# Attention times V on four 64x64 quarters in two turns, and a new order on every engine

## The reference

```python
q = rmsnorm((x @ wq.T).reshape(B, T, 16, 64), q_norm_w)
k = rmsnorm((x @ wk.T).reshape(B, T, 4, 64), k_norm_w);  v = (x @ wv.T).reshape(B, T, 4, 64)
scores = einsum('bqhd,bkhd->bhqk', q, repeat(k, 4)) / 8
mask = (i >= j) & (i - j < 128)
y = einsum('bhqk,bkhd->bqhd', softmax(where(mask, scores, -inf)), repeat(v, 4))
x = x0 + y @ wo.T                      # x above is layernorm(x0)
x = x + base(layernorm(x)) + gated_lora(layernorm(x))
```

## Time and profile before

| | |
|---|---|
| median of 3 runs | 2423.83 us (2421.53 to 2424.13) |
| profiled execution, its own time | 2420.27 us |
| its span, first to last instruction | 2418.6 us |
| TensorE, VectorE, ScalarE, GpSimd busy | 2380.1, 2152.0, 2160.9, 1309.6 us |
| granted TensorE clock, mean | 0.996 |
| bytes moved | 41.23 MB, mean 17 GB/s |

### The profile page before, as it was taken

The page is one execution under the profiler, slowest core; times in us unless marked ns, Lnnn a source line. Parts: engine busy times, 40 slices in busy tenths (PEclk is TensorE's granted clock), DMA queues, the critical chain, the costliest instruction groups (busy, mean ns, idle before and its releaser), DMA issues.

```text
span 2418.6 us, 70409 instructions
## 1 busy us (share of the span) xinstructions
PE 2380.1 (98%) x25856; PEld 1958.6 (81%) x25856; DVE 2152.0 (89%) x5736; ACT 2160.9 (89%) x7687; POOL 1309.6 (54%) x1771
## 2 busy tenths in 40 slices
PE   6999999999999999999999999999999999999997
PEld 4888888888888888888888888888888888888886
DVE  6899899999988999999999899989999998999886
ACT  5899989999998999899989989998999899899996
POOL 3555555555555555555555555555555555555542
PEclk9999999999999999999999999999999999999999
DMA  2000000000000000000000000000000000000000
GB/s 70 13 15 19 15 15 16 18 15 15 19 15 15 15 19 15 15 15 19 15 15 19 16 15 15 19 15 15 15 20 15 15 17 18 15 15 19 13 9 12
DMA packets 39729, 41.23 MB, mean 17 GB/s; under 512 B 4448, under 2 KB 38624, under 8 KB 39392
## 3 DMA queue, kind: packets, MB, share of 16 engines
q1 hardware_dynamic: 39392, 36.73, 5.0%
HBM read 19.93 MB, written 16.78 MB: 15 GB/s over the span
## 4 chain that ended last, share of the span: by engine, by line
PE 97%; issue 1%; ACT 1%; POOL 1%; DVE 1%; DMA 0%; SPq 0%; POOLq 0%
PE ps_a L633 17%; PE ps_scores L676 14%; PE ps_y L695 12%; PE ps_d L629 7%; PE ps_d L627 7%; PE ps_d L628 7%; PE ps_y L710 5%; PE ps_b L629 5%; PE ps_b L627 5%; PE ps_b L628 5%; PE ps_d L633 3%; PE ps_c L629 2%; PE ps_c L628 2%; PE ps_c L627 2%; PE ps_c L633 1%
## 5 line engine op out<-in xcount | busy, mean ns | idle before, releaser
L330 ACT ACTIVATE probs<-merged,neg_max 128x128 f32<-128x128 f32 x2048 | 796.0, 394 | 0.5 <-DVE neg_max L491 0.5
L253 POOL TENSOR_SCALAR_AFFINE_SELECT pT_other<-pT 128x256 f32<-128x256 f32 x384 | 173.1, 451 | 606.4 <-ACT pT L345 606.4
L237 POOL TENSOR_TENSOR q_r<-q_ve,minus_half 128x8 f32<-128x8 f32 x256 | 420.3, 1642 | 92.4 <-DVE q_ve L467 92.4
L676 PE MATMUL ps_scores<-kT,qT 64*64 64x192 f32 (+2 forms) x8192 | 415.2, 311 | 1.0 <-DVE merged L481 0.6
L330 ACT ACTIVATION_READ_ACCUMULATOR probs<-merged,neg_max 128x1 f32 x2048 | 396.5, 194 | 0.0
L481 DVE COPY_PREDICATED merged<-later_key,ps_scores 128x512 f32<-128x512 int32 x384 | 284.7, 741 | 106.2 <-ACT merged L323 106.2
L345 ACT ACTIVATE pT<-ps_a 128x512 f32<-128x512 f32 x512 | 306.2, 598 | 62.0 <-PE ps_a L633 61.1
L491 DVE TENSOR_REDUCE neg_max<-merged 128x4 f32<-128x512 f32 x512 | 346.5, 677 | 4.5
L695 PE MATMUL ps_y<-pT,values 128*64 128x128 f32 x4096 | 337.0, 285 | 1.8 <-ACT pT L345 1.8
L633 PE MATMUL ps_a<-ident,probs 128*128 128x128 f32 x2048 | 336.4, 287 | 0.0
L676 PEld LDWEIGHTS ps_scores<-kT,qT 64*64 64x64 f32 x8192 | 262.7, 133 | 60.6 <-issue 32.8
(11 more groups left out here) (114 smaller groups left out, 6175.7 us busy)
## 6 DMA issues: line engine op xcount, KB each, us to landing
xs<-x SPq DMA_DIRECT2D x128, 128.0 KB, 2.2
out<-ob SPq DMA_DIRECT2D x128, 128.0 KB, 1.7
w_plain<-w_qkv SPq DMA_DIRECT2D x3, 512.0 KB, 5.0
w_plain<-w_o SPq DMA_DIRECT2D x8, 128.0 KB, 5.3
w_plain<-w_ffn SPq DMA_DIRECT2D x1, 392.0 KB, 5.7
w_plain<-w_v SPq DMA_DIRECT2D x1, 128.0 KB, 4.9
nw<-norm_w SPq DMA_DIRECT2D x1, 1.0 KB, 5.5
```

The costliest lines, as they stand in the source:

```text
L237: pool.tensor_tensor(q_r[:, T % DEEP, c], q_ve[:, T % DEEP, c], minus_half[:, 0:8], ALU.pow).then_inc(s_qr[n], 1)
L330: last = nc.scalar.activation(probs[:, r, h], merged[:, r, h], ACT.Exp, bias=neg_max[:, r, h:h + 1], accum_out=den[:, r, h:h + 1])
L676: last = nc.tensor.matmul(ps_scores[queries, 2 * half + c, first:end], qT[rows, T % 2, 2 * g + c, queries], kT[rows, g // 2, at + first:at ...
```

## The change

The product with V is cut finer. What was one pass over 128 keys (`attend`) is now two turns of four matmuls over 64 keys, each on one quarter of the array: `attend_across`, the keys of the half that lies across from the queries' half, and `attend`, the keys of the same half. The first turn starts the sums in `ps_y`, then come the scores of a group of the next tile, then `attend` and `attend_other`, in one order or the other. The two later ones wait for the new semaphore `s_px`, which the first turn's last matmul raises. The number of multiplications is the same, the number of matmuls of L695 doubles.

```diff
-            def attend(T, g, first=True):
+            def attend_across(T, g):
                 pe.wait_ge(s_pT, groups(T, g))
...
-                for n in range(2):
-                    for half in range(2):
-                        last = nc.tensor.matmul(ps_y[HD * half:HD * half + HD, n, 0:P], values[:, T % WIDE, g // 2 * 2 + half],
-                                                pT[:, ring(T, g), 2 * half:2 * half + 2, HD * n:HD * n + HD], start=first, stop=ends, skip_group_check=True)
+                for half in range(2):
+                    for n in range(2):
+                        keys = slice(HD - HD * n, P - HD * n)
+                        last = nc.tensor.matmul(ps_y[HD * half:HD * half + HD, n, 0:P], values[keys, T % WIDE, g // 2 * 2 + half],
+                                                pT[keys, ring(T, g), 2 * half:2 * half + 2, HD * n:HD * n + HD], start=True, stop=False, skip_group_check=True)
+                last.then_inc(s_px, 1)
+
+            def attend(T, g, last=False):
+
+                pe.wait_ge(s_px, groups(T, g))
+                ends = last or not slot(T)
+                for half in range(2):
+                    for n in range(2):
+                        keys = slice(HD * n, HD * n + HD)
+                        end = nc.tensor.matmul(ps_y[HD * half:HD * half + HD, n, 0:P], values[keys, T % WIDE, g // 2 * 2 + half],
+                                               pT[keys, ring(T, g), 2 * half:2 * half + 2, HD * n:HD * n + HD], start=False, stop=ends, skip_group_check=True)
```

The lists of all five engines are new, the small PSUM banks are handed out anew, and the drain has one more step on TensorE. Of these lists two lines of VectorE and SyncE's loop:

```diff
-        ps_q, ps_qT = [ps_d, ps_c], [ps_d, ps_a]
-        ps_kv, ps_kT, ps_xT, ps_hT, ps_tT = ps_b, ps_a, ps_d, ps_a, ps_c
+        ps_q, ps_qT = [ps_d, ps_c], [ps_b, ps_a]
+        ps_kv, ps_kT, ps_xT, ps_hT, ps_tT = ps_c, ps_b, ps_a, ps_a, ps_a
...
-            for T in range(TILES):
+            for T in range(TILES + 2):
                 load_x(T + WIDE)
-                sp.wait_ge(s_ob, done(T))
-                sp.dma_start(out[T * P:(T + 1) * P, :], ob[:, T % 2]).then_inc(s_st[T % 2], 16)
+                store(T - 2)
...
-                x_statistics(T + 4)
...
+                add_x(T - 1)
+                x_statistics(T + 7)
```

More of the change, by code:

```diff
@@ L170, in load_x, with store @@
                     sp.dma_start(xs[:, T % WIDE], x[T * P:(T + 1) * P, :]).then_inc(s_x[T % WIDE], 16)
+            def store(T):
+                if live(T):
+                    sp.wait_ge(s_ob, done(T))
+                    sp.dma_start(out[T * P:(T + 1) * P, :], ob[:, T % 2]).then_inc(s_st[T % 2], 16)
             def load_weight(n):
@@ new lines, in step @@
+                norm_probs(T, 0)
+                k_mean_square(T + 1)
+                low_x(T + 2)
+                maximum(T, 2)
+                norm_h(T - 2)
+                inverse(T, 1)
+                norm_k(T + 1)
+                x_mean_and_var(T + 6)
+                low_y(T - 1, 3)
+                merge(T, 3)
+                norm_probs(T, 1)
+                maximum(T, 3)
+                inverse(T, 2)
+                sum_q(T + 1, 1)
+                low_h(T - 2)
+                q_mean_square(T + 1, 1)
@@ L618, in _ @@
+                add_x(T - 1)
+                x_statistics(T + 7)
+                h_statistics(T - 1)
+                high_value_difference(T + 1)
+                if T == -1:
+                    low_weights(W_FFN, W_O, W_V)
+                merge(T + 1, 0)
+                low_y(T, 0)
             low_weights(0, 1, 2)
@@ L709, in attend_other @@
                         keys = slice(HD * n, HD * n + HD)
-                        last = nc.tensor.matmul(ps_y[HD * half:HD * half + HD, n, 0:P], v_diff[keys, T % RING, g // 2 * 2 + half],
-                                                pT_other[keys, ring(T, g), n, 2 * half:2 * half + 2], start=first, stop=not first, skip_group_check=True)
-                if not first:
-                    last.then_inc(s_pv, 1)
+                        end = nc.tensor.matmul(ps_y[HD * half:HD * half + HD, n, 0:P], v_diff[keys, T % RING, g // 2 * 2 + half],
+                                               pT_other[keys, ring(T, g), n, 2 * half:2 * half + 2], start=False, stop=last, skip_group_check=True)
+                if last:
+                    end.then_inc(s_pv, 1)
             def project_out(T, g):
@@ new lines, in step @@
+                if live(T - 1):
+                    freed(pe, (s_merged, T - 1, groups(T - 1, 1)))
+                    scores(T - 1, 2)
+                if live(T - 2):
+                    attend(T - 2, 2)
+                if live(T - 2):
+                    attend_other(T - 2, 2, last=True)
+                if live(T - 2):
+                    freed(pe, (s_ttl, T - 4, done(T - 4)), (s_qT[1], T - 1, done(T - 1)), (s_pT, T - 2, groups(T - 2, 2)))
+                    transpose_probs(T - 2, 3)
@@ new lines, in step @@
+                if live(T - 2):
+                    freed(pe, (s_yl, T - 2, groups(T - 2, 2)))
+                    attend_across(T - 2, 3)
+                if live(T - 1):
+                    freed(pe, (s_merged, T - 1, groups(T - 1, 2)))
+                    scores(T - 1, 3)
+                if live(T - 2):
+                    attend_other(T - 2, 3)
+                if live(T - 2):
+                    attend(T - 2, 3, last=True)
+                if live(T):
+                    freed(pe, (s_ob, T - 4, done(T - 4)), (s_kT, T - 1, done(T - 1)), (s_qT[0], T - 1, done(T - 1)))
+                    transpose_q(T, 0)
```

225 lines of the change are left out of this document (90 added, 135 removed).

## The result

| | before | changed |
|---|---|---|
| median of the runs | 2423.38 us (4 runs, 2421.53 to 2424.13) | 2488.22 us (4 runs, 2486.7 to 2491.68) |
| ratio | | 1.0271, 95% interval 1.0253 to 1.0289 |
| span of the profiled execution | 2418.6 us | 2485.0 us |
| granted TensorE clock, mean | 0.996 | 0.996 |

A forecast was written before the change was run, and what follows sets the result against it. VectorE, with 17.06 us of need plus a 2.3 us load wait per tile, was to replace TensorE as bound: 2420.3 + 102.6 - 4.8 = 2518, plus 3.6 to the median, 2522 us; eighty per cent range 2488 to 2565.

The forecast's parts named there:

- The cause and the sign: VectorE's statistics wait 2.3 us for the load add_x just released, 120 times, 276 us; kernel slower, 95%.
- TensorE's term: Each group's place costs 1.47 us instead of 1.62, 77 us in 512 places; TensorE alone needs 17.9 us per tile.
- The new order of the other matmuls: On TensorE, transposes and projections in their new order, with as many passages between kinds, cost nothing.
- All rivals on TensorE: Quarters not four at a time in the turns, 2572 us, 3%; idle TensorE with lowered clock, up to 2650 us, 9%.
- the price of one change of the array's shape: On TensorE, one change of shape fewer in each group's place saves 0.15 us.
- The mechanism that turned the wait into time: VectorE becomes the bound by its own work plus the load's wait, 19.35 us per tile against 18.495 before; 83%.
- VectorE's need: VectorE needs 17.06 us per tile when nobody keeps it waiting: 16.72 busy plus 0.34 of short gaps.
- the slack: VectorE's spare time against TensorE's 17.9 us per tile, 0.84 us, is all that can hide the load's wait.
- the forecast's own range: For the whole kernel with VectorE as bound: 19.1 to 19.65 us per tile, 2492 to 2558 us.
- the wider one: The eighty per cent range for the whole kernel's time, 2488 to 2565 us.
- The cover of `s_px`: On TensorE the scores cover the wait for s_px by 0.47 us; uncovered it would cost about 0.15 us.

The follow-up runs named there:

- x_ring9: The changed kernel with nine x buffers instead of eight, nothing else changed: 2344.36 us, ratio 0.9682 to the kernel before.
- x_stats_late: The changed kernel, still eight x buffers, with x_statistics(T + 7) called later, behind low_y(T, 0): 2347.29 us, ratio 0.9695 to the kernel before.
- halves_new: The changed kernel with twelve x buffers and the product with V as before, one pass over 128 keys: 2417.09 us, ratio 0.9979 to the kernel before.
- x_ring12: The changed kernel with twelve x buffers instead of eight, nothing else changed: 2344.7 us, ratio 0.9684 to the kernel before.
- norm_h_pool: The changed kernel with norm_h, 0.33 us of VectorE work per tile, moved to GpSimd: 2491.25 us, ratio 1.0282 to the kernel before.
- halves_wait: The changed kernel, eight x buffers, with the product with V as before, one pass over 128 keys: 2536.7 us, ratio 1.0475 to the kernel before.
- before_scores: x_ring12 with the scores moved behind both turns, so nothing covers the wait for s_px: 2509.13 us, ratio 1.0357 to the kernel before.
- split: The changed kernel, eight x buffers, with each load of x as two DMAs of 64 partitions: 2582.86 us, ratio 1.0665 to the kernel before.
- old_with_stall: The kernel before with x_statistics right behind add_x, six x buffers and SyncE's stores two tiles later: 2751.82 us, ratio 1.1376 to the kernel before.

## Why the prediction was right, and where it was not

**The cause and the sign were right.** The statistics waited for a load 121 times, 274.9 us (one of them at the start of the kernel), against 120 times and 276 us predicted for the load that their neighbour releases. x_ring9 and x_stats_late show that this wait is the whole loss.

**TensorE's term was right.** A place costs 1.47 us; a tile 17.90 us without the wait; 72 us from the quarters by halves_new against x_ring12, and 77 us for the whole kernel against the one before. The new order of the other matmuls, costed at nothing, gave 5 us. All rivals on TensorE fell: quarters run four at a time, and the clock stayed at 1.00 in the steady stretch with about 1 us of idle TensorE in each tile. That the 0.15 us are the price of one change of the array's shape is read from the starts, which all came as that reading says; no run varied the number of changes by itself.

**The mechanism that turned the wait into time was wrong.** The step that failed is "So VectorE becomes the bound: 17.06 + 2.3 = 19.35 us per tile". Two things were off in it. VectorE's need was too large: 17.06 was busy time before plus its short gaps, but its busy time is 16.23 us per tile now, with the same instructions, and the gaps 0.28, so 16.51. With 2.26 for the load this makes 18.77, less than the 19.075 measured. And the bound is not VectorE's sum but the cycle over TensorE and ScalarE, which leaves VectorE waiting another 0.30 us per tile for `q_sq`: 37 us less work on VectorE changed nothing (norm_h_pool), 77 us more on TensorE, which the prediction would have called hidden, cost 48.5 (halves_wait). The two errors have opposite signs. What they add up to is the slack: 0.84 us per tile in the prediction, an estimated 1.1 to 1.2 by the runs. The loss per tile against TensorE's 17.9 was thus 1.2 us instead of 1.45, and the time 2488 instead of 2522 us.

That is below the forecast's own range (2492 to 2558 us) and inside the wider one (2488 to 2565) by 0.2 us. That the number fits at all is partly luck: with VectorE's need put right and the bound left as it was, the same sum gives 120 x (18.77 - 18.495) - 4.8 + 2423.9 = 2452 us, and the cycle that the prediction did not see makes up the rest.

**The cover of `s_px`** was right, its price without cover wrong by a factor of two: 0.32 us instead of 0.15. The sum did not use it.

**Of what the profile was to show**, these failed: VectorE's busy time near 2150 us (it was 2091.1), its idle time almost all of one kind (0.30 us per tile was for `q_sq`), and 1.4 us of idle TensorE per tile. TensorE was idle 2136.42 - 2026.60 = 109.8 us in 112 tiles, 0.98 each.

The Trainium skill ("DMA: Bandwidth & Descriptors", section "Rules for kernel authors") advises to issue a DMA early, compute, and wait for it late. The changed kernel did the reverse, and x_stats_late, with the later call as its only edit, gains 141 us: the trace agrees.

## What to carry to other kernels

When a list of instructions is reordered, look at each wait for a DMA and ask what releases the buffer that this DMA writes: if the releasing instruction stands just ahead of the waiting one on the same engine, the full landing time is paid on each turn, and one more buffer or a later call removes it. The price of such a wait is not read from the engine that waits. Follow the chain from one such wait to the next: what lies on this cycle costs, on whatever engine, and what lies beside it is free even on the engine that stalls. Follow it over several turns, since here three tiles of four took another way than the first one that was looked at.

A change of a data path (here the quarters) and a change of order should be timed apart as well as together: the quarters were worth 72 us in one order and 28 in the other, and the bundle was a loss only for the place of one call, which has nothing to do with the quarters.

## What the runs showed that was not expected

- TensorE's wait for a semaphore that its own matmul raises cost 0.32 us beyond the spacing of 0.27 (before_scores), though the records of the awaited matmuls end 0.45 us after the first starts.
- VectorE's busy time for the same instructions is not a constant: 16.23 us per tile in the changed kernel and 1839.59 / 112 = 16.42 in x_ring12, against 16.72 in the earlier trace rows. It does not follow the time of a tile (19.07, 17.90 and 18.5 us), and why it differs stays open.
- A load of 64 KB landed no sooner than one of 128 KB (2.2 and 2.1 us in the median), and the second of two in a row was issued later: the statistics waited 0.72 us longer per tile for what was meant to be a split of one transfer (split).
- The same 2.2 us wait cost 1.2 us per tile in one order and 2.6 in another (old_with_stall), more than its own length.
